# A two-part graph network on one core: settling stages fed from the attentions ahead, records saved and reloaded, marks joined on TensorE

## The chip, the cores and the metric

The kernel runs on one core of one Trainium2 chip. The metric is the device time of one execution in microseconds (us). Engines are named as the profile names them: PE is TensorE, DVE is VectorE, ACT is ScalarE, POOL is GpSimd, SP is SyncE, which here only issues transfers.

## What is computed

x has 1250 rows of 768 numbers, the graph 20000 edges (src, dst, one of 34 types). The first part is a network of two GATv2 layers (eight heads, then one), the second a relational layer with an ordinary graph convolution behind it:

```python
def gatv2(x, src, dst, Ws, bs, Wd, bd, attn):
    H, D = attn.shape
    fs = (x @ Ws + bs).reshape(-1, H, D)
    fd = (x @ Wd + bd).reshape(-1, H, D)
    e = leaky_relu(fs[src] + fd[dst], 0.2)
    logits = einsum('ehd,hd->eh', e, attn)
    alpha = softmax of logits over the edges of one dst
    out = segment_sum(alpha[:, :, None] * fs[src], dst, num_segments=N)
    return elu(out)
...
h0 = relu(layernorm(x))
h = layer_norm(gatv2(h0, first weights) + h0, ln1_w, ln1_b)
x = x + layer_norm(gatv2(h, second weights), lno_w, lno_b)
h = relu(layernorm(x))
mean[r, n] = mean of h[src] over the edges of type r into n
h1 = sum over r of mean[r] @ W_rel[r] + h @ W_root + b_rgcn
x = x + gcn(h1 @ W_gcn) + b_gcn
```

## The kernel before, in words

The nodes are ranked by degree and stand in NT = 10 tiles of 128 rows. The edges of a tile are worked off in groups: a group is S = 4 edges for each of 128 nodes. There are 48 groups in 12 turns of U = 4, and three more at the ends whose slots are empty. The kernel is a chain of stages with a barrier between them (`stage`); each engine has its own instruction stream, and semaphores order the streams inside a stage.

1. **Sorting and projection** (up to 323 us): ranks, edge records in `by_dst_d`, then fs and fd for the first layer. Marks of the (type, source) pairs that occur are scattered into four DRAM tables `marked_d`, in part here, in part in the first settling stage (`mark`, L520 to L526).
2. **First attention** (`attention`, L826, from 323.8 us). POOL first gathers all ten tiles of fd (L884), waits for them, and then runs `gather_edges` (L754): it makes `next`, `step` and `slot`, fetches the records of three groups (`record`, L768 to L773), the rows of two (`rows`, L775 to L778), and goes into its loop of turns, which gathers the record of group u+3 and then the four row sets of group u+2. VectorE clears its tables (L977 to L985), adds fs and fd (`add`, L990), makes the softmax arguments (`arguments`, L1033, first line L1041) and the weights; ACT sums and scales; TensorE adds rows (L942, L944) and sums weighted rows (L965).
3. **First settling stage** (`settle(True)`, L1304). SP loads two layer norm vectors, attr and two biases by broadcast to all partitions, then two weights (L1403 to L1410). VectorE waits for all five vectors (L1565) before anything else. For each of ten tiles it divides by the denominators (`rden`, L1622), takes the smaller of this and 0 (L1626), lets ACT make the exponential, adds (L1629), adds h0, normalises (L494 to L503, L1643 to L1647); TensorE transposes and multiplies (L480, L487), VectorE adds the bias. `twice` (L1388) orders the tiles. POOL gathers and scatters the rows and sets 60 of the 160 marks.
4. **Single attention** (`attention_single`, L1089). The same with one head; VectorE counts the edge types per node too (`count`, L1268), and a Signal `read` tells POOL when a record may be overwritten (L1272, L807).
5. **Second settling stage** (`settle(False)`). VectorE waits for four vectors (L1565), makes `rden` (L1568), the counts per type (L1577 to L1581), waits for the four mark tables (L1583), joins them by three maxima (L1585), makes a running sum (L1586) and from it the tables of the relation stage, with two trips to TensorE (L1545 to L1549) and a store of `seen_d` by SP. Then come the ten tiles. A tile has one `o`, `low`, `y` and `mv`; the next one starts behind it (L1619). It has two normalisations: L503 ends each; after the second ACT copies y (L1515), makes the ReLU (L1518) and copies the transposes (L1522), and VectorE adds the bias to the product (L1681).
6. **Relations** (1942 to 2943 us) and **aggregation** (`gather_edges` with `keep_ends`, L2008): rows of y_d are gathered by edge; POOL casts the records to `ends` (L799), VectorE makes weights from them (L2088 to L2109) and adds weighted rows (L2115).
7. **Last stage**: product, graph convolution, output.

## Time and profile before

| | us |
|---|---|
| median of 3 runs | 3665.88 (3660.69 to 3670.1) |
| the profiled execution | 3660.05 |
| its span, from the first to the last instruction | 3658.2 |
| PE busy | 2852.5 (78%) |
| DVE busy | 2403.2 (66%) |
| ACT busy | 1807.4 (49%) |
| POOL busy | 1770.9 (48%) |
| mean granted TensorE clock | 0.889 of full |

The page of the profile gives busy time by engine, the span in 40 slices, the costliest groups of instructions and the chain that ended last. In a kernel of stages such sums are averages over parts with different limits, so the rows further down are from single stages. A line of a timeline is: start, duration, engine, line of the kernel, operation, output and inputs, count, and in brackets how long the engine was idle before it and what released it. "issue" stands for time in which the engine waited for nothing that the profile shows.

### The profile page before, as it was taken

Reading aid. Unit: us, or ns where it says so; the run is one execution under the profiler, and the core shown is the slowest. Engines: PE = TensorE matmul, PEld = TensorE weight load, DVE = VectorE, ACT = ScalarE, POOL = GpSimd, SP = SyncE. Lnnn points to the kernel's source line nnn. Section 1 sums busy time; section 2 is a strip of 40 time slices with the busy share of each in tenths; the row PEclk is TensorE's granted clock in tenths of the full one; section 3 lists DMA queues with packets and bytes.
Section 4 is the critical chain, followed back from the end, with each engine's and each line's share of the span. In section 5 each row is a group of like instructions: output and inputs, shape, how many; then the busy total and the mean of one; then the engine's idle time right before and its main releaser. Section 6 shows DMA issues by size and latency. Waiting matters only on the chain. (4 is left out here: it accounts for less than half of the span.)

```text
span 3658.2 us, 59690 instructions
## 1 busy us (share of the span) xinstructions
PE 2852.5 (78%) x12846; PEld 2109.5 (58%) x12847; DVE 2403.2 (66%) x4964; ACT 1807.4 (49%) x5370; POOL 1770.9 (48%) x2270
## 2 busy tenths in 40 slices
PE   0495888888779799997476999999999934444699
PEld 0253444444445455553246999999999924444455
DVE  5233988898766788887564655555555569999312
ACT  0011888888722122221243656565566648888300
POOL 1574454544446666664012554455444557777000
PEclk6797999999989899999678999999999966666899
DMA  1334444443321455555126777777776545555200
GB/s 34 111 95 133 125 122 122 122 122 122 117 88 44 149 157 157 157 157 157 47 77 208 241 246 249 231 237 245 245 237 228 187 149 177 174 173 176 105 13 29
DMA packets 153631, 545.35 MB, mean 149 GB/s; under 512 B 35106, under 2 KB 36118, under 8 KB 153281
## 3 DMA queue, kind: packets, MB, share of 16 engines
q0 software_dynamic: 85344, 371.14, 32.6%
q1 hardware_dynamic: 47938, 127.49, 10.7%
q10 hardware_dynamic: 20304, 46.21, 4.0%
q8 instruction: 17, 0.28, 0.0%
q14 instruction: 28, 0.23, 0.0%
HBM read 461.45 MB, written 83.59 MB: 149 GB/s over the span
## 5 line engine op out<-in xcount | busy, mean ns | idle before, releaser
L1921 PE MATMUL pO<-wh,gT 128*128 128x384 f32 x3264 | 867.4, 339 | 15.5 <-ACT gT L1872 13.6
L777 POOL DMA_INDIRECT row<-fs_d,rec x400 | 443.3, 1108 | 351.2 <-PE pA L965 188.2
L1921 PEld LDWEIGHTS pO<-wh,gT 128*128 128x128 f32 x3264 | 594.8, 189 | 24.0 <-ACT gT L1872 20.5
L1921 PE MATMUL pO<-wl,gT 128*128 128x384 f32 x1632 | 547.7, 336 | 0.0
L487 PE MATMUL pO<-wt,hT 128*128 128x384 f32 (+1 forms) x1200 | 417.9, 510 | 40.9 <-ACT hT L1522 19.6
L1935 DVE TENSOR_SCALAR cntge<-pT 128x768 int32<-128x768 int32 x137 | 131.2, 958 | 421.4 <-PE pT L480 231.2
L2044 PE MATMUL pC<-identb,own 128*128 128x128 bf16 x960 | 193.8, 305 | 233.7 <-DVE counts L2074 107.4
L903 ACT ACTIVATE sj<-sj 128x96 f32<-128x96 f32 x1176 | 313.1, 268 | 100.0 <-DVE sj L1020 98.4
L487 PEld LDWEIGHTS pO<-wt,hT 128*128 128x128 f32 (+1 forms) x1200 | 235.7, 199 | 213.4 <-issue 65.9
L1872 ACT ACTIVATE gT<-cntge 128x256 fp32r<-128x256 f32 x822 | 296.8, 411 | 32.0 <-DVE cntge L1938 4.3
L1921 PEld LDWEIGHTS pO<-wl,gT 128*128 128x128 f32 x1632 | 308.3, 189 | 0.0
L942 PE MATMUL pS<-row,ident 128*128 128x384 f32 x400 | 184.5, 546 | 128.3 <-DVE sj L1020 90.3
L1198 PE MATMUL pA<-row,share 128*128 128x384 f32 x768 | 256.3, 487 | 0.0
L2044 PEld LDWEIGHTS pC<-identb,own 128*128 128x128 bf16 x960 | 115.2, 143 | 243.5 <-issue 67.7
L965 PE MATMUL pA<-row,ident 128*128 128x384 f32 x768 | 255.5, 486 | 0.0
L777 POOL DMA_INDIRECT row<-y_d,rec x200 | 211.6, 1058 | 66.5 <-issue 61.2
L2022 ACT ACTIVATE far<-nrow,source 128x1280 bf16<-128x1280 f32 x144 | 196.1, 1362 | 90.3 <-DMA row<-y_d,rec 43.6
L525 POOL DMA_INDIRECT marked_d<-marks,recc x160 | 200.0, 1250 | 68.5 <-issue 56.6
L1797 POOL DMA_INDIRECT g<-hr_d,gindex x138 | 168.2, 1219 | 121.6 <-POOL keys L1794 59.0
L903 ACT ACTIVATION_READ_ACCUMULATOR sj<-sj 128x1 f32 x1176 | 220.0, 187 | 2.4 <-issue 2.2
L772 POOL DMA_INDIRECT rec<-by_dst_d,index x153 | 188.2, 1230 | 47.0 <-issue 30.9
L1198 PEld LDWEIGHTS pA<-row,share 128*128 128x128 f32 x768 | 146.7, 191 | 102.8 <-issue 2.0
(351 smaller groups left out, 5837.0 us busy)
## 6 DMA issues: line engine op xcount, KB each, us to landing
fdt<-in_L_gnn_W_rel_dram SPq DMA_DIRECT2D x170, 384.0 KB
startrow<-seen_d ACTq DMA_DIRECT2D x141, 320.0 KB
raw<-in_L_gnn_W_rel_dram SPq DMA_DIRECT2D x34, 384.0 KB
row<-fs_d,rec POOLq DMA_INDIRECT x400
kept_d<-fdt SPq DMA_DIRECT2D x10, 384.0 KB
kept<-kept_d SPq DMA_DIRECT2D x1, 3840.0 KB
fs_d<-of SPq DMA_DIRECT2D x9, 388.0 KB
fd_d<-of SPq DMA_DIRECT2D x9, 388.0 KB, 2.7
```

The lines of the kernel that those rows point to most:

```text
L487: last = pe.matmul(dst[0:rows, q, 0:HALF], rows_t[:, c * P:c * P + rows], w[:, c, lo:up], start=c == 0, stop=c == KC - 1)
L525: pool.indirect_dma_start(marked_d[k], bass.IndirectOffsetOnAxis(ap=keys, axis=0), marks[0:EP], None)\
L772: pool.indirect_dma_start(b["rec"][u][:], None, table_rows, bass.IndirectOffsetOnAxis(ap=b["index"][u][:], axis=0)).then_inc(b["rec_in"][u ...
L777: pool.indirect_dma_start(b["row"][u][:, j, :].bitcast(words), None, table, bass.IndirectOffsetOnAxis(ap=b["rec"][u][:, 2 * j + field:2 * ...
L903: last = act.activation(of_head, of_head, ACT.Copy, accum_out=dots[off % U][:, j, h:h + 1])
L942: pe.matmul(pS[j][:, q, 0:HALF], ident[:], row[off % U][:, S // 2 + j, lo:up], start=True, stop=False)
L965: last = pe.matmul(pA[:, q, 0:HALF], share, row[u][:, j, lo:up], start=j == 0, stop=j == S - 1)
L1198: last = pe.matmul(pA[u % 2][:, q, 0:HALF], share[u % 2][:, 1 + j, :], row[u][:, j, lo:up], start=j == 0, stop=False)
L1872: act.activation(gT[:, c].bitcast(F32R), cut[:, :, c * P:(c + 1) * P], ACT.Copy).then_inc(gT_ok.sem, 1)
L1921: last = pe.matmul(pO[:, q, 0:HALF], gT[:, c, half, :].bitcast(F32R), w[:, c, lo:up].bitcast(F32R), start=c == 0 and k == 0, stop=c == KC ...
L2022: act.activation(far[:], of_node[:], ACT.Square, bias=source[u % 2][:, j:j + 1], scale=-1.0)\
L2044: last = pe.matmul(pC[u % 2][:, c // 4, (c % 4) * P:(c % 4 + 1) * P], equal[u % 2][j][:, c * P:(c + 1) * P], identb[:], start=j == 0, stop ...
```

## The change

- **Ahead.** A new class holds a weight (768 x 768) and two layer norm vectors in SBUF. SP loads them behind its other work in the attention; the settling stage that follows uses them. The first gets Wos, ln1_w and ln1_b, the second W_root, lno_w and lno_b.
- **fd.** In the first attention POOL gathers tile 0 of fd first, the other nine behind the first eight row gathers.
- **Records.** `gather_edges` is split. In the first attention SP writes each group's record to `groups_d` (`save_records`); in the single attention and the aggregation SP reads them from there (`load_records`), and POOL gathers rows only (`gather_rows`). POOL's casts to `ends` are gone; VectorE reads the integer records and signals `read`.
- **settle** is written out as `settle_first` (as before, but for the loads) and `settle_last`.
- **settle_last.** Two sets of `o`, `low`, `y`, `mv`. VectorE starts the next tile inside the present one and evacuates the one before at its end. The four mark tables are joined by accumulating matmuls with the identity on TensorE and a Sign on ACT, between tile 0 and tile 1. The running sum, the tables and the counts stand behind the tiles on VectorE.

The diff, cut to its core:

```diff
+        groups_d = dram("groups_d", (MAX_TURNS * U + U - 1, P, S * 2), I32)
...
+        def gather_edges(pool, b, table, used, between):
+            count_slots(pool, b)
...
             for u in range(ROWS_AHEAD):
                 pool.wait_ge(b["rec_in"][u], 16)
-                rows(u)
-            turns = pool.value_load(ctl[0:1, C_TURNS:C_TURNS + 1], min_val=1, max_val=MAX_TURNS)
+                rows_of(pool, b, u, table, 0, F32)
+            between()
+            turns = turns_of(pool)
...
                     rows_wait(pool, b, i, u - 1)
-                    if read is not None:
-                        read.wait(pool, i, u - 1)
+                    pool.wait_ge(b["saved"][w], i * 16 + 16 * ((u + U - 1) // U))
...
+        def save_records(sp, b):
+            turns = turns_of(sp)
+            with sp.Fori(0, turns) as i:
+                for u in range(U):
+                    sp.wait_ge(b["rec_in"][u], i * 16 + 16)
+                    sp.sem_inc(b["sp_posted"], 1)
+                    sp.dma_start(groups_d[ds(i * U + u, 1)].rearrange("o p c -> p (o c)"), b["rec"][u][:]).then_inc(b["saved"][u], 16)
...
+        def load_records(sp, b):
+            for u in range(U - 1):
+                sp.dma_start(b["rec"][u][:], groups_d[u]).then_inc(b["rec_in"][u], 16)
+            turns = turns_of(sp)
+            with sp.Fori(0, turns) as i:
+                for u in range(U):
+                    rows_wait(sp, b, i, u - 1)
+                    sp.sem_inc(b["sp_posted"], 1)
+                    b["read"].wait(sp, i, u - 1)
+                    sp.sem_inc(b["sp_posted"], 1)
+                    w = u + U - 1
+                    sp.dma_start(b["rec"][w % U][:], groups_d[ds(i * U + w, 1)].rearrange("o p c -> p (o c)"))\
+                      .then_inc(b["rec_in"][w % U], 16)
...
+        def gather_rows(pool, b, table, field, used, words=F32):
+            count_slots(pool, b)
...
+                for u in range(U):
+                    w = u + ROWS_AHEAD
+                    pool.wait_ge(b["rec_in"][w % U], i * 16 + 16 * (w // U + 1))
+                    used.wait(pool, i, w - U)
+                    pool.sem_inc(b["posted"], 1)
+                    rows_of(pool, b, w % U, table, field, words)
...
+        class Ahead:
...
+            def load(self, sp):
+                weight, lnw, lnb = (io[n] for n in self.names)
+                sp.dma_start(self.wt[:], w_view(weight)).then_inc(self.w_in, 16)
+                sp.dma_start(self.lnw[:], lnw.partition_broadcast(P)).then_inc(self.v_in, 16)
+                sp.dma_start(self.lnb[:], lnb.partition_broadcast(P)).then_inc(self.v_in, 16)
...
                         sp.dma_start(attr[:], attn.rearrange("h d -> (h d)").partition_broadcast(P)).then_inc(att_in, 16)
+                        save_records(sp, b)
+                        ahead.load(sp)
...
-                            for t in range(NT):
-                                pool.indirect_dma_start(fdt[:, t, :], None, fd_table, bass.IndirectOffsetOnAxis(
-                                    ap=permc[:, t:t + 1], axis=0)).then_inc(fd_in, 16)
-                            pool.wait_ge(fd_in, 16 * NT)
-                        pool.sem_inc(init_ok, 1)
-                        gather_edges(pool, b, fs_d[0:N], 0, summed)
+                        def others():
+                            for t in range(1, NT):
+                                fd_rows(t)
+                        fd_rows(0)
+                        gather_edges(pool, b, fs_d[0:N], summed, others)
...
                         add(0, 0, 0)
+                        pe.wait_ge(init_ok, 1)
+                        pe.wait_ge(fd_in, 16 * (NT - 1))
...
-                        dve.wait_ge(init_ok, 2)
+                        dve.wait_ge(fd_first, 16)
...
                         add(0, 0, 0)
+                        dve.wait_ge(fd_in, 16 * (NT - 1))
                         turns = dve.value_load(ctl[0:1, C_TURNS:C_TURNS + 1], min_val=1, max_val=MAX_TURNS)
...
+                        load_records(sp, b)
+                        ahead.load(sp)
                         sp.wait_ge(att_in, 16)
...
-                        gather_edges(pool, b, fs_d[0:N], 0, summed, read=read)
+                        gather_rows(pool, b, fs_d[0:N], 0, summed)
```

In `settle_first` SP loads attr, the two biases and Wod only; VectorE waits for them ahead of its first evacuation, TensorE for Wod ahead of its second product. `settle_last`, by engine:

```diff
+                        for k in range(MARKS):
+                            sp.dma_start(marked[:, k, :], marked_d[k].rearrange("(r s) o -> r (s o)", r=RELS)).then_inc(present_in, 16)
+                        sp.dma_start(bias[:], io["L1_gnn_b_rgcn"].partition_broadcast(P)).then_inc(b_in, 16)
...
+                        def rows(i, b):
+                            root(i, b, 2)
+                            affine_ok.wait(act, i, b)
+                            act.activation(ht[b][:], y[b][:], ACT.Relu, bias=mv[b][:, 3:4], scale=mv[b][:, 2:3])\
+                               .then_inc(h_ok.sem, 1)
+                            act.activation(of_tile(fdt, i, b)[:, 0:D], y[b][:], ACT.Copy).then_inc(kept_ok.sem, 1)
+                            t_ok.wait(act, i, b)
+                            prod_ok.wait(act, i, b - 2)
+                            act.activation(split(hT[b][:]), halves(pT), ACT.Copy).then_inc(hT_ok.sem, 1)
...
+                        exp(0, 0)
+                        tile(0, 0, (0, 1))
+                        act.wait_ge(summed, 1)
+                        act.activation(marked[:, 0, :], p_join[0:RELS].rearrange("p q f -> p (q f)")[:, 0:NP], ACT.Sign)\
+                           .then_inc(joined, 1)
...
+                        pe.wait_ge(present_in, 16 * MARKS)
+                        for q, lo, up in ((0, 0, 512), (1, 512, 1024), (2, 1024, NP)):
+                            for k in range(MARKS):
+                                last = pe.matmul(p_join[0:RELS, q, 0:up - lo], ident[0:RELS, 0:RELS], marked[:, k, lo:up],
+                                                 start=k == 0, stop=k == MARKS - 1)
+                        last.then_inc(summed, 1)
+                        turn(0, 0)
...
+                        product(4, 0)
+                        turn(4, 1)
+                        pe.wait_ge(rel_const, 6)
+                        pe.wait_ge(ntiles_ok, 1)
+                        pe.matmul(p_ends[0:RELS, RELS:RELS + 1], upto[:], ntiles[:], start=True, stop=True)
+                        pe.matmul(p_ends[:, 0:RELS], ntiles_all[:], upto[:], start=True, stop=True).then_inc(ends_ok, 1)
+                        product(4, 1)
+                        pe.wait_ge(behind_ok, 1)
...
+                            row_stats(dve, v, y[b], stats, mv[b], P)
+                            dve.sem_inc(var_ok.sem, 1)
...
+                                begin(v, *following)
+                            root_ok.wait(dve, i, b, 1)
...
+                            if behind is not None:
+                                evacuate(*behind)
...
+                        with dve.Fori(0, 4) as i:
+                            tile(i, 1, (i + 1, 0), (i, 0))
+                            tile(i + 1, 0, (i + 1, 1), (i, 1))
+                        tile(4, 1, None, (4, 0))
+                        dve.wait_ge(joined, 1)
+                        pre.link(dve.tensor_tensor_scan(seen_keys, marked[:, 0, :], marked[:, 0, :], 0.0, ALU.add, ALU.max))
```

And in the aggregation:

```diff
-                    gather_edges(pool, b, y_d, 1, used, keep_ends=True, words=I32)
+                    gather_rows(pool, b, y_d, 1, used, words=I32)
...
-                            b["valid"].wait(dve, i, u)
+                            dve.wait_ge(b["rec_in"][u], i * 16 + 16)
...
                             v.link(dve.tensor_tensor(ge[:], over(ends[:, :, 1], 2, shape),
                                                      over(relbase[:], 1, shape), ALU.is_ge))
+                            dve.sem_inc(b["read"].sem, 1)
                             v.link(dve.tensor_tensor(of_rel[:], ge[:, :, 0:RELS], ge[:, :, 1:RELS + 1],
                                                      ALU.subtract))
```

## Rows read from the trace of the kernel before

**Rows 1.** Busy us by stage, columns PE, PEld, DVE, ACT, POOL, then clock, DMA share, GB/s
```profile
323.80:996.30 672.50, 549.23 (x1568) 309.20 (x1568) 579.02 (x1169) 555.22 (x3180) 333.91 (x366) 0.93 0.41 125
...
1201.50:1718.10 516.60, 458.94 (x1360) 259.55 (x1360) 439.48 (x1365) 137.88 (x349) 327.12 (x356) 0.96 0.53 155
...
1718.10:1942.60 224.50, 116.47 (x308) 66.24 (x308) 127.89 (x240) 62.57 (x79) 26.97 (x48) 0.73 0.21 75
```

**Rows 2.** Timeline, start of the first attention: start us, us, engine, line, idle before
```profile
323.82 1.00 POOL L884 DMA_INDIRECT fdt<-fd_d,permc  x1 [38.69 <-POOLq L139]
...
339.84 0.19 POOL L760 COPY next<-first_row 128x11 int32<-128x11 int32 x1 [3.72 <-DMA fdt<-fd_d,permc]
...
340.24 0.17 DVE L977 COPY left<-degr 128x11 f32<-128x11 f32 x1 [21.11 <-POOLq L765]
...
346.30 0.95 POOL L777 DMA_INDIRECT row<-fs_d,rec  x1 [0.31 <-issue]
...
354.58 1.83 DVE L1001 TENSOR_TENSOR sj<-row,fdt 128x768 f32<-128x768 f32 x2 [2.00 <-DMA row<-fs_d,rec]
...
365.58 0.23 DVE L1041 TENSOR_SCALAR neg<-slot,left 128x4 f32<-128x4 f32 x1 [1.20 <-ACT sj L903]
```

**Rows 3.** Timeline, end of the first attention and start of the first settling stage
```profile
966.45 0.98 POOL L772 DMA_INDIRECT rec<-by_dst_d,index  x1 [0.47 <-issue]
...
988.78 5.32 PE L965 MATMUL pA<-row,ident 128*128 128x384 f32 x16
...
996.28 0.36 SPq L1403 DMA_DIRECT2D lnw<-in_L_gnn_ln_w_dram  x1
...
1008.44 0.20 DVE L1568 TENSOR_SCALAR rden<-den 128x80 f32<-128x80 f32 x1 [13.07 <-DMA bias<-in_L_gnn_bod_dram]
```

**Rows 4.** Timeline of the single attention, VectorE, its start and a turn's start
```profile
1216.56 1.83 DVE L1232 TENSOR_TENSOR leak<-row,fdt 128x768 f32<-128x768 f32 x2 [0.22 <-DMA row<-fs_d,rec]
...
1468.53 0.23 DVE L1254 TENSOR_SCALAR val<-slot,left 128x4 f32<-128x4 f32 x1 [1.51 <-issue]
```

**Rows 5.** Waits, 1240 to 1700 us: who waited for what, us in total, times, longest
```profile
PE pS L1180 <- DMA row<-fs_d,rec: 34.1, 36, 2.3
```

**Rows 6.** Timeline of the second settling stage, its start and its last tile
```profile
1727.55 0.17 DVE L1568 TENSOR_SCALAR rden<-den 128x10 f32<-128x10 f32 x1 [16.48 <-DMA bias<-in_L_gnn_b_rgcn_dram]
...
1734.19 1.22 SPq L1420 DMA_DIRECT2D marked<-marked_d  x4
...
1749.93 4.52 DVE L1585 TENSOR_TENSOR marked<-marked 34x1280 f32<-34x1280 f32 x3 [15.04 <-DMA marked<-marked_d]
...
1754.49 2.82 DVE L1586 TENSOR_TENSOR_SCAN startrow<-marked 34x1280 f32<-34x1280 f32 x1
...
1762.22 1.20 PE L1549 MATMUL p_tile<-behind,ntiles_all 34*128 34x300 f32 x2
...
1765.26 0.96 DVE L1622 TENSOR_TENSOR o<-acc,rden 128x768 f32<-128x768 f32 x1
...
1911.91 0.96 DVE L1622 TENSOR_TENSOR o<-acc,rden 128x768 f32<-128x768 f32 x1 [0.95 <-ACT ht L1518]
...
1916.51 0.96 DVE L1629 SCALAR_TENSOR_TENSOR o<-o,low 128x768 f32<-128x768 f32 x1 [3.04 <-ACT low L1508]
...
1926.27 0.16 DVE L503 SCALAR_TENSOR_TENSOR mv<-mv 128x1 f32<-128x1 f32 x1
...
1930.78 9.91 PE L487 MATMUL pO<-wt,hT 128*128 128x384 f32 x24 [0.90 <-ACT hT L1522]
...
1940.73 0.96 DVE L1681 TENSOR_TENSOR acc<-pO,bias 128x768 f32<-128x768 f32 x1 [13.19 <-PE pO L487]
```

**Rows 7.** Timeline of the aggregation, VectorE, within one group of edges
```profile
3201.98 0.89 DVE L2098 TENSOR_SCALAR own<-nrow,source 128x1280 bf16<-128x1280 f32 x1 [0.16 <-DVE source L2096]
3202.78 0.30 DVE L2101 TENSOR_TENSOR ge<-ends,relbase 128x140 f32<-128x140 f32 x1
3203.11 0.30 DVE L2103 TENSOR_TENSOR of_rel<-ge 128x136 f32<-128x136 f32 x1
```

653 lines of the change are left out of this document (378 added, 275 removed).

## The prediction

> **What bounds the kernel now.** I read the page first, for the loops, then the busy times stage by stage, then the timeline at each border between stages, and last the waits inside the loops.
>
> Busy times by stage [rows 1]: VectorE works 579 of 672 us in the attention of eight heads and 439 of 517 us in the single one, but only 128 of 224.5 us in the second settling stage, where TensorE works 116. That stage is bound by a chain that passes between engines, not by an engine.
>
> Borders. The first attention begins with ten gathers of fd, a wait for them, then the records and rows; VectorE's first addition comes 30.8 us after the first gather, and the softmax of the first group 11.0 us later [rows 2]. The first settling stage opens with a VectorE wait of 13.07 us for the broadcast vectors [rows 3]. The second opens with the same wait (VectorE's first work is at 1727.55), then waits 15.04 us for the marks, and starts its first tile at 1765.26 [rows 6]. From there a tile takes (1911.91 - 1765.26)/9 = 16.3 us [rows 6].
>
> Inside the single attention the only wait on VectorE that lasts is 1.51 us of register loads, once a turn of four groups [rows 4]. TensorE waits for rows [rows 5], but has time left.
>
> **The change, part by part.** The profiled execution took 3660.05 us, span 3658.2; the median of the runs shown is 3665.88. The sum is against 3660, and I apply it to the median. What a measurement can tell from no change is 0.3%, 11 us.
>
> *fd behind the first rows.* POOL issued ten gathers from 323.82 to 336.12, where its wait begins, one each 1.23 us. With one fd gather ahead, the slot numbers are ready at about 325.4 in place of 340.0; VectorE's memsets last 12.3 us (340.24 to 352.58, where its wait for rows begins) and end at about 338.1. POOL repeats 339.84 to 354.58 (14.7 us from the first copy to the rows being there) from about 325.6, so the first addition comes at 340.3, 14.3 us sooner [rows 2]. But nine fd gathers follow the eight of rows: eight begin at 332.1, nine at 342.1, issued by 353.1, and landed 3.7 us later, as in the row of L760: 356.8. VectorE waits for them ahead of its turn loop, behind which stand the softmax arguments of group 0 and all that ACT and TensorE do for it; its register loads (1.5 us) come behind that wait. So the softmax starts at 358.3 in place of 365.58: **-7.3**. Bounds: -14.3 if the loads and the wait hide, -4 if the seventeen gathers land more slowly than issued. POOL reaches its loop 3 us sooner, and group 2's rows keep their lead.
>
> *Saving the records.* SP writes 51 records of 4 KB; POOL waits for that before it overwrites a buffer whose record came several us earlier. VectorE sets this loop, POOL does not (334 of 672 us busy [rows 1]): 0, and at most 51 issues' worth of POOL's spare time. The weights wait on SP behind the last save: the last record is gathered at 966.45 [rows 3], so they leave at about 972, 24 us before the stage ends; late next would be the last row gather, if they crowd it.
>
> *First settling stage.* VectorE waits for nothing at its start. SP begins at 996.28; VectorE's six semaphore openings take some 0.8 us, so 997.1 in place of 1008.44: **-11.3** [rows 3]. What is late next: three broadcasts and Wod, 3.5 MB. At the pace of the five vectors before (2 MB by 1008.44) they are there by 1018, and TensorE wants Wod only behind a first tile and a first product, 12 and 10 us as in [rows 6], about 1022. The gather of h0's rows has 4 us less cover, so I leave -8 to -12. The tiles behind run as before.
>
> *Single attention.* POOL loses per group two small operations and a record gather, SP gets a load and two waits. VectorE's own loop is unchanged. At the start, memsets and rows end together (VectorE waits 0.22 us for rows [rows 4]), and the memsets stay: **0**, between -2 and +2.
>
> *Second settling stage.* The first tile no longer waits for broadcasts, marks or tables: VectorE starts it at 1720, not 1765.26. Tile 0 takes at most the 14.5 us of the last one (1911.91 to the end of L503, 1926.43). Then, in tile 1, it stalls. ACT's queue holds, between tile 0 and tile 1, the copy of tile 0's transposes and the Sign of the joined marks; TensorE does the join first. Four mark loads are there 15.7 us after their issue (1734.19 to 1749.93), so at 1733.9. The join is 12 matmuls over 5120 columns [rows 6]: at the pace of the last product (12 x 384 columns in 9.91 us, begun on an idle TensorE) 11.0 us; at the pace of L1549 (300 columns in 1.20 us) 20.5; at that of L965 (8 x 384 columns in 5.32 us [rows 3]) 8.9. L1549 ran behind an idle TensorE and L965 in a busy stretch, 4.0 and 1.7 ns a column: near the two levels of the granted clock, 1.2 and 2.4 GHz, whose mean is 0.73 of full in this stage [rows 1]. I take 12, nearest to the product, which gives 1746; transposes, copy and Sign add 3.9 (my estimate, from the 4.35 us between L503 and the last product, which hold two copies, a ReLU and the transposes): 1749.9. Tile 1 has two thirds of its 9.9 us left from there: 1756.5. For the period: 9.9 us from L1629 to the end of L503 (1916.51 to 1926.43), the next tile's first two operations 1.6 (1911.91 to 1916.51, less 3.04 of wait), evacuation 1.0, less the 0.3 wait for the root, and 0.7 of semaphore and register work: 12.9 us, against 16.3. The last product (9.9 us) has to fit behind the way through ReLU, transposes and copy, 4.35 us less the 0.8 of the other copy, which now stands behind; that makes 13.5, so it just fails to fit at half clock and fits at the full one. Eight tiles less one opening: 101.5, so 1858. Then the tables, once ahead of the tiles, stand behind them: 10.8 us from the scan to the first tile (1754.49 to 1765.26), with TensorE's last product, 9.9, and two evacuations put in between, less 1 that overlaps; VectorE's count sums (7.3 us, 1727.55 to 1734.89, with the reciprocal of the denominators) lie beside that product. End at 1879.5 in place of 1941.7: **-62**. Bounds: -74 (full clock) and -40 (join at 20.5 and a period of 14.5).
>
> *Aggregation.* POOL's casts go; they were not what VectorE waited for. VectorE gets one more semaphore increment per group. Such an increment stands ahead of L2098: VectorE is idle 0.16 us there, against 0.03 between the end of L2101 and L2103, where none stands [rows 7]. VectorE has no other idle time there, so 48 x 0.13 = **+6**; bounds 0 and +8. The Trainium skill, VectorE: DVE Perf Modes, The DRAIN you can't avoid, says a semaphore after each operation costs nothing extra. By that rule this term would be 0 and the sum 6 us lower. It speaks of increments carried by an operation, and the row of a separate one disagrees.
>
> Sum: -7.3 - 11.3 - 62 + 6 = -74.6: 3585.5 against 3660.05, 3591 on the median.
>
> **The rivals.**
> *Less overlap.* Two tiles share one pT and one pO, and ACT and TensorE take their work in order. If that holds the period at 15 to 16.3 us, eight tiles cost 17 to 27 more: about 3616. For it: the product nearly fails to fit. Against: each wait I can follow is met with a us to spare.
>
> *The rows set the single attention.* TensorE waited 34.1 us for rows in 460 us [rows 5], and POOL's next record waits for VectorE's read. If that drives VectorE, freeing POOL gives up to 34: 3557. Against: VectorE's waits don't name rows, sums or TensorE [rows 4]. The Trainium skill, SBUF — State Buffer, SBUF: two separate sides, says a gather issued by GpSimd can't write its descriptors while VectorE holds the port they share. The record loads leave that path for SP's, so by this rule too the way to the rows gets shorter.
>
> *Slower.* Both later gather loops now get their records from SP, behind two waits and a round trip through DRAM in 32-byte pieces. If a record comes later than POOL wants it by d per group, 96 groups pay 96 d; the gain is gone at d = 0.78 us, and d = 1.5 gives 3735. For it: it is a new wait in front of every row gather. Against: a record is asked for a whole group, 9 to 10 us, before its rows are. The Trainium skill, DMA: Bandwidth & Descriptors, Specifications, warns of transfers under 512 bytes, handled by read-modify-write; by this rule SP's 4 KB writes would be slow, but no row here shows a price.
>
> *The prefetch doesn't land.* If SP is still held by its last waits when the attention ends, both settling stages load as before: 11 us lost in the first and up to 8 in the second: 3605.
>
> **How the numbers follow.** Forecast as summed 0.62 (3591), less overlap 0.15 (3616), rows 0.07 (3557), prefetch late 0.08 (3605), slower 0.04; 0.04 for two small losses at once that leave no measurable change. The forecast's own bounds add up to about -95 and -45 if all fall one way; independent ones to some -88 and -52. The range 3563 to 3625 takes in the forecast, less overlap and late prefetch, and leaves out the slow rival and the far end of the rows. Faster by over 0.3%: 0.92; within: 0.04; slower: 0.04.
>
> **What would show it.** In the profile after: VectorE's first addition at about 340 and softmax at 358; no wait for a broadcast at either settling start; between tiles 0 and 1 of the second a VectorE wait of 9 to 11 us for ACT's root; a tile period near 12.9 us; TensorE's last product between the two table matmuls; the single attention as long as before; aggregation 6 us longer, with 0.16 us behind L2101's successor. A tile period over 15 us, row waits on VectorE, or POOL waiting for records would prove me wrong.

## The result and the profile after

The kernel after took 3608.39 us (median of 4 runs, 3602.33 to 3609.28) against 3667.99 us of the kernel before (4 runs, 3660.69 to 3671.18): a ratio of 0.9837, with a 95% interval of 0.9818 to 0.9856. That is 59.6 us less; the prediction was 75 less (3591, range 3563 to 3625), so the measured time lies 17 us above the forecast and inside its range. The profiled execution took 3608.54 us with a span of 3606.6; the one before, 3660.05, was the shortest of its runs, so the two profiles differ by 51.6 us and not by 59.6. What follows splits those 51.6.

Busy times by stage in the kernel after (columns as in [rows 1]: PE, PEld, DVE, ACT, POOL, clock, DMA share, GB/s): first attention, single attention, second settling stage.

```profile
323.87:999.61 675.74, 556.18 (x1568) 312.11 (x1568) 578.88 (x1169) 554.28 (x3180) 338.38 (x366) 0.92 0.43 129
1197.00:1714.85 517.85, 461.29 (x1360) 261.11 (x1360) 440.99 (x1365) 135.39 (x349) 233.27 (x200) 0.96 0.55 161
1714.85:1890.60 175.75, 123.86 (x332) 65.43 (x332) 119.54 (x237) 63.59 (x80) 25.61 (x46) 0.78 0.22 74
```

The second settling stage does the same work in 175.75 us that took 224.5. The two attentions are as long as they were, though GpSimd does 94 us less in the single one. The account, from the timelines of both kernels:

| part | before, us | after, us | difference | predicted |
|---|---|---|---|---|
| first attention, first fd gather to last addition | 671.55 | 674.77 | +3.2 | -7.3 |
| from there to the first work of the single attention | 207.21 | 199.24 | -8.0 | -11.3 |
| single attention | 515.52 | 516.97 | +1.5 | 0 |
| second settling stage | 224.5 | 175.75 | -48.8 | -62 |
| relations, up to the clearing of the counts | 1004.4 | 1003.6 | -0.8 | 0 |
| aggregation, to its last addition of counts | 465.36 | 466.59 | +1.2 | +6 |
| the rest | | | 0 | 0 |

**Start of the first attention.** The timeline answers to [rows 2]; the last row is of TensorE.

```profile
323.87 1.00 POOL L956 DMA_INDIRECT fdt<-fd_d,permc  x1 [39.56 <-POOLq L141]
340.80 1.83 DVE L1079 TENSOR_TENSOR sj<-row,fdt 128x768 f32<-128x768 f32 x2 [3.35 <-DMA row<-fs_d,rec]
360.23 0.23 DVE L1119 TENSOR_SCALAR neg<-slot,left 128x4 f32<-128x4 f32 x1 [9.49 <-issue]
363.20 0.27 DVE L1130 COPY top<-mnew 128x8 f32 x1 [1.19 <-issue]
368.17 0.96 DVE L1079 TENSOR_TENSOR sj<-row,fdt 128x768 f32<-128x768 f32 x1 [4.71 <-issue]
379.25 0.23 DVE L1119 TENSOR_SCALAR neg<-slot,left 128x4 f32<-128x4 f32 x1 [0.20 <-issue]
...
358.99 1.62 PE L1018 MATMUL pS<-row,ident 128*128 128x384 f32 x2 [11.09 <-issue]
```

The first addition is 13.8 us sooner, the softmax arguments of group 0 are 5.4 us sooner, and those of group 1 come later than before, at 379.25 against

```profile
378.30 0.23 DVE L1041 TENSOR_SCALAR neg<-slot,left 128x4 f32<-128x4 f32 x1 [0.20 <-issue]
```

TensorE stood 11 us at the same wait for the nine gathers as VectorE and did its sums for group 1 only from 358.99, beginning at half clock; before, it had done them while VectorE was still on group 0. VectorE then stops twice (1.19 and 4.71 us) where nothing in the trace releases it. TensorE's sums are ready at 367.2, before VectorE comes back at 368.17, so in this profile the stops took the lead and not the late sums.

**End of the first attention**, answering to [rows 3]:

```profile
985.10 0.91 PE L1018 MATMUL pS<-row,ident 128*128 128x384 f32 x2 [3.79 <-DMA row<-fs_d,rec]
...
992.05 5.32 PE L1043 MATMUL pA<-row,ident 128*128 128x384 f32 x16
997.68 0.96 DVE L1108 TENSOR_TENSOR acc<-pA,scaled 128x768 f32 x1 [7.65 <-PE pA L1043]
999.61 0.33 SPq L1457 DMA_DIRECT2D attr<-in_L_gnn_attno_dram  x1
1000.21 0.20 DVE L1388 TENSOR_SCALAR rden<-den 128x80 f32<-128x80 f32 x1 [1.56 <-PEq L141]
1008.58 0.96 DVE L1584 SCALAR_TENSOR_TENSOR y<-o,hg 128x768 f32<-128x768 f32 x1 [2.23 <-DMA hg<-h_d,gindex]
```

The last group's 16 matmuls start at 992.05 in place of 988.78. The settling stage then starts 0.6 us behind its border with no broadcast to wait for, and waits 2.23 us for the gathered rows of h0.

**Second settling stage**, answering to [rows 6]:

```profile
1714.85 1.24 SPq L1675 DMA_DIRECT2D marked<-marked_d  x4
1716.23 0.72 DVE L1828 TENSOR_SCALAR o<-acc,rden 128x768 f32<-128x768 f32 x1
1734.36 17.28 PE L1797 MATMUL p_join<-marked,ident 34*34 34x512 f32 x24 [21.42 <-DMA marked<-marked_d]
1736.29 0.96 DVE L1841 SCALAR_TENSOR_TENSOR o<-o,low 128x768 f32<-128x768 f32 x1 [5.23 <-DMA bias<-in_L_gnn_b_rgcn_dram]
...
1753.15 0.81 ACT L1758 ACTIVATE hT<-pT 128x768 f32<-128x768 f32 x1 [20.23 <-PE pT L482]
1753.85 1.22 ACT L1772 ACTIVATE marked<-p_join 34x1280 f32<-34x1280 f32 x1
1755.20 0.17 DVE L504 RECIPROCAL mv<-mv 128x1 f32<-128x1 f32 x1 [13.98 <-ACT mv L1744]
1763.84 0.96 DVE L1834 TENSOR_TENSOR acc<-pO,bias 128x768 f32 x1 [2.09 <-PE pO L489]
...
1857.13 0.96 DVE L1834 TENSOR_TENSOR acc<-pO,bias 128x768 f32 x1 [0.28 <-DVE mv L505]
1871.55 0.96 DVE L1834 TENSOR_TENSOR acc<-pO,bias 128x768 f32<-128x768 f32 x1 [3.54 <-PE pO L489]
1876.88 9.64 PE L489 MATMUL pO<-settle_wt,hT 128*128 128x384 f32 x24
1886.64 0.96 DVE L1834 TENSOR_TENSOR acc<-pO,bias 128x768 f32<-128x768 f32 x1 [1.76 <-PE pO L489]
```

VectorE starts its tiles at once. In tile 1 it waits 13.98 us for ScalarE's root, because the root stands behind the copy of tile 0's transposes and the Sign, and these stand behind the join on TensorE: 17.28 us. After that the evacuations are (1857.13 - 1763.84)/7 = 13.3 us apart, and the last product lies between the two table matmuls.

**Waits for rows** on TensorE in the single attention, 1236 to 1696, answering to [rows 5]:

```profile
PE pA L1279 <- ACT share L1245: 28.9, 16, 3.9
PE pS L1261 <- DMA row<-fs_d,rec: 5.4, 9, 1.7
```

Of the 34.1 us for rows 5.4 are left. 28.9 us for ScalarE stand in the place of the rest.

### The profile page after: what moved, and what is told of

It is laid out like the page before. It is cut to its first block and busy times, and to the rows that moved or that the text cites. A ratio compares the mean times of both kernels' runs of the same rounds, so it can differ in the third digit from the quotient of the medians.

```text
span 3606.6 us, 59098 instructions
## 1 busy us (share of the span) xinstructions
PE 2867.7 (80%) x12870; PEld 2109.7 (58%) x12871; DVE 2393.1 (66%) x4961; ACT 1802.2 (50%) x5371; POOL 1545.8 (43%) x1910
## 5 line engine op out<-in xcount | busy, mean ns | idle before, releaser
L759 POOL DMA_INDIRECT row<-y_d,rec x200 | 202.9, 1014 | 248.9 <-DVE acc L2343 198.9
L1279 PE MATMUL pA<-row,share 128*128 128x384 f32 x768 | 265.6, 500 | 30.7 <-ACT share L1245 30.7
L489 PE MATMUL pO<-wt,hT 128*128 128x384 f32 (+1 forms) x720 | 238.3, 490 | 22.1 <-DMA attr<-in_L_gnn_attn_dram 12.9
L489 PEld LDWEIGHTS pO<-wt,hT 128*128 128x128 f32 (+1 forms) x720 | 135.7, 190 | 119.4 <-issue 31.4
L1043 PEld LDWEIGHTS pA<-row,ident 128*128 128x128 f32 x768 | 145.9, 190 | 101.8
```

The lines of the kernel that those rows point to most:

```text
L489: last = pe.matmul(dst[0:rows, q, 0:HALF], rows_t[:, c * P:c * P + rows], w[:, c, lo:up], start=c == 0, stop=c == KC - 1)
L759: pool.indirect_dma_start(b["row"][u][:, j, :].bitcast(words), None, table, bass.IndirectOffsetOnAxis(ap=b["rec"][u][:, 2 * j + field:2 * ...
L1043: last = pe.matmul(pA[:, q, 0:HALF], share, row[u][:, j, lo:up], start=j == 0, stop=j == S - 1)
L1279: last = pe.matmul(pA[u % 2][:, q, 0:HALF], share[u % 2][:, 1 + j, :], row[u][:, j, lo:up], start=j == 0, stop=False)
```

## The experiments

Every kernel below is the kernel after with the edit named. Whole times scatter: the one with fd gathered ahead gave 3605 to 3625 in four runs, and the relations, whose code is the same everywhere, took between 1006 and 1016 us. So verdicts rest on lengths of stages, each from one profile. These scatter too: where the second settling stage has the same code, "settling 2" took 171.1 to 174.7 us in eight profiles, "single" 512.7 to 520.1 in all of them. The column "start" runs from the first fd gather to the softmax arguments of group 1, "attention" to the last addition, "settling 1" from there to its last copy of fd, "single" from the first work of that attention to the first work of the next stage, and "settling 2" from there to the start of its last evacuation (for the kernel before counted from 0.5 us behind SP's first issue, as in the others).

| kernel | start | attention | settling 1 | single | settling 2 | aggregation | median, us | ratio to before (95%) |
|---|---|---|---|---|---|---|---|---|
| before | 54.5 | 671.6 | 204.9 | 516.0 | 222.1 | 465.4 | | |
| after | 55.4 | 674.8 | 197.0 | 517.5 | 171.3 | 466.6 | 3608.4 | 0.9837 |
| after, again | 56.3 | 672.4 | 196.8 | 517.9 | 173.7 | 466.5 | 3609.0 | 0.9849 (0.9824-0.9873) |
| fd ahead | 59.4 | 676.1 | 196.5 | 519.4 | 171.9 | 466.4 | 3619.2 | 0.9864 (0.9839-0.9889) |
| no prefetch | 54.9 | 673.0 | 203.8 | 513.7 | 174.3 | 466.7 | 3617.0 | 0.9870 (0.985-0.989) |
| join on VectorE | 56.7 | 674.7 | 197.3 | 517.4 | 156.7 | 466.2 | 3600.2 | 0.9826 (0.981-0.9843) |
| own records | 57.0 | 675.5 | 196.6 | 516.9 | 171.5 | 465.4 | 3612.8 | 0.9854 (0.9838-0.9871) |
| two fd rows ahead | 42.8 | 665.1 | 196.5 | 518.0 | 174.0 | 466.7 | 3600.4 | 0.9827 (0.9811-0.9844) |
| join on VectorE, bias first | 50.0 | 667.9 | 197.2 | 513.2 | 157.0 | 466.2 | 3589.1 | 0.9803 (0.9786-0.9821) |
| nothing saved | 49.9 | 668.3 | 196.9 | 516.7 | 174.7 | 464.7 | 3604.0 | 0.9839 (0.9816-0.9862) |
| join warmed up | 50.0 | 668.0 | 197.0 | 520.1 | 168.4 | 466.4 | 3605.5 | 0.9843 (0.9823-0.9863) |
| tiles kept warm | 56.3 | 672.6 | 196.4 | 516.9 | 150.3 | 466.1 | 3586.0 | 0.9788 (0.976-0.9816) |
| earlier prefetch | 58.1 | 674.1 | 195.8 | 512.7 | 171.1 | 466.1 | 3608.1 | 0.9851 (0.9819-0.9883) |
| all three | 50.7 | 669.1 | 196.9 | 514.0 | 150.7 | 468.0 | 3586.5 | 0.9785 (0.9764-0.9805) |

**1. fd gathered ahead of the records again.**

```diff
 fd_rows(0)
-gather_edges(pool, b, fs_d[0:N], summed, others)
+others()
+pool.wait_ge(fd_first, 16)
+pool.wait_ge(fd_in, 16 * (NT - 1))
+gather_edges(pool, b, fs_d[0:N], summed, lambda: None)
```

> The kernel after, with all ten rows of fd gathered ahead of the records, as in the kernel before. My theory: the lead of 14.5 us that the new order gives at the first addition (340.8 against 354.6) is lost before the second group is done, because TensorE, VectorE and ScalarE stand behind one wait for the nine other gathers (until about 358) and start again on cold queues; VectorE then reaches the softmax of group 1 at 379.25 against 378.30 in the kernel before. So undoing it costs nothing: first addition at 354.6, softmax of group 0 at 365.6, softmax of group 1 at about 378.3, and a time within 2 us of the kernel after (3606 to 3610). Rival: the new order does give its 7.3 us and the loop loses them later to the saving of the records; then the stage ends 7 us later than in the kernel after and the time is about 3615.

The start took 59.4 us, 4 us more than in the kernel after, not the same; the stage ended 1.3 us later, not 7. Neither forecast holds, and the time, 3619.2 us, is above both. The new place of fd does give something, but 59.4 is also 4.9 more than the kernel before had with the same order of gathers, and here too VectorE stopped 3.22 us without a releaser. So the next question was the saving.

**2. Nothing saved.** No records are written; both later loops gather their own (experiment 6 has that part alone).

```diff
-pool.wait_ge(b["saved"][w], i * 16 + 16 * ((u + U - 1) // U))
...
-sp.dma_start(groups_d[ds(i * U + u, 1)].rearrange("o p c -> p (o c)"), b["rec"][u][:]).then_inc(b["saved"][u], 16)
```

> The kernel after, but no records are saved: the single attention and the aggregation gather their own, and in the first attention SP writes nothing and GpSimd waits for no save; the prefetch leaves when the last record is there. The fd gathers stand as in the kernel after. From the first fd gather to the softmax of group 1 the kernel before took 54.5 us, the kernel after 55.4, and the one with fd gathered ahead and records saved 59.4. My theory: the saving costs about 4 us at the loop's start (its writes of 32 bytes a partition go through the same DMA engines as the first rows and the engines' code) and the new place of fd gives about as much back; without the saving the softmax of group 1 comes 50 to 52 us after the first fd gather. Rival: the saving costs nothing; then it stays at 55 to 57.

49.9 us, at the lower edge of my theory's window, and yet the theory falls: two kernels that ran beside it on the same chip and save every record (join on VectorE with the bias first, join warmed up) had 50.0. There, saving costs nothing. The first of the two shows the start without the stops, against the same lines of the kernel after above:

```profile
360.83 0.23 DVE L1119 TENSOR_SCALAR neg<-slot,left 128x4 f32<-128x4 f32 x1 [9.49 <-issue]
...
363.08 1.83 DVE L1079 TENSOR_TENSOR sj<-row,fdt 128x768 f32<-128x768 f32 x2 [0.30 <-issue]
374.72 0.23 DVE L1119 TENSOR_SCALAR neg<-slot,left 128x4 f32<-128x4 f32 x1 [0.20 <-issue]
```

Its wait for fd is as long (9.49 us), but the first pass through the loop runs on. Here VectorE does wait for TensorE's late sums, 1.07 us. Where the stops are absent, the new place of fd gives 54.5 - 50.0 = 4.5 us. Where they are present it gives 59.4 less about 56.4 = 3, a weak reading: 59.4 is one profile, and the seven others with stops have starts from 54.9 to 58.1. Whether a kernel that saves nothing would have them on the chips that show them was not tried.

**3. Two rows of fd ahead, the wait for the other eight inside the loops.**

```diff
-.then_inc(fd_first if t == 0 else fd_in, 16)
+.then_inc(fd_first if t < 2 else fd_in, 16)
...
 add(0, 0, 0)
-dve.wait_ge(fd_in, 16 * (NT - 1))
...
 arguments(v, i, u, t[u + 1])
+if u == 1:
+    dve.wait_ge(fd_in, 16 * (NT - 2))
 add(i, u + 1, t[u + 2])
```

(and the same for TensorE, ahead of its sums for the third group)

> The kernel after, but two rows of fd are gathered ahead of the records and eight behind the first rows, and the wait for those eight stands inside the loops, ahead of the addition of the third group, not ahead of the loops. My theory: the wait ahead of the loops holds three engines until about 358; with it gone the softmax of group 0 starts about 353 (first addition 342, plus 11 as in the kernel before), the softmax of group 1 at about 366 to 368 against 379.25, and the lead stays to the end of the stage: 8 to 11 us off the first attention. Rival: the loop's start is held by the crowd of gathers itself (the operations behind it show idle times of 4.7 and 1.2 us without a releaser), not by the wait; then the softmax of group 1 stays at 376 or later and the stage gives 3 us or less.

The start took 42.8 us, 7.2 less than the kernels beside it and as forecast: the wait ahead of the loops was the cost. But the stage is only 2.9 us shorter (665.1 against 668.0), where I had forecast 8 to 11. The rest is lost one group later, on TensorE and VectorE:

```profile
366.88 1.64 PE L1019 MATMUL pS<-row,ident 128*128 128x384 f32 x2 [10.68 <-DMA row<-fs_d,rec]
...
375.15 0.96 DVE L1100 SCALAR_TENSOR_TENSOR sj<-pS,attr 128x768 f32<-128x768 f32 x1 [1.48 <-PE pS L1021]
380.42 0.96 DVE L1110 TENSOR_TENSOR acc<-pA,scaled 128x768 f32 x1 [2.46 <-PE pA L1045]
```

The rows of the third group are gathered behind the eight of fd, and TensorE takes them up at half clock. A queue of 25 gathers of about 1.25 us each has to be worked off in any order.

**4. No prefetch in the first attention.**

```diff
 save_records(sp, b)
-ahead.load(sp)
...
 def _(sp):
+    ahead.load(sp)
...
```

> The kernel after, but the first Wos and the two norm vectors are loaded at the start of the first settling stage and not behind the saved records. My theory: the 2.9 MB of the prefetch crowd the last row gather of the attention; in the kernel after TensorE waits 3.79 us for it (985.10 against 983.51) and then runs at half clock, so the stage ends at 999.6 against 996.3. Without the prefetch TensorE takes up the last group at 983.5 and the stage ends 3.3 us sooner, at 996.3; the settling stage then waits 5 to 10 us for vectors and weights, so the time is 2 to 7 us above the kernel after (3610 to 3615). Rival: the late end comes from the saving of the records, not from the prefetch; then the stage still ends at 999.6 and the time is 5 to 10 us above.

The settling stage took 203.8 us, 6.8 more; VectorE waits 9.95 us in it for a norm vector. The time, 3617.0 us, is 2 above my forecast. The end of the attention did not come back to that of the kernel before: TensorE's wait was 2.22 us, as before, but it went on at half clock all the same:

```profile
985.46 1.65 PE L1017 MATMUL pS<-row,ident 128*128 128x384 f32 x2 [2.22 <-DVE sj L1097]
986.90 1.49 PE L1019 MATMUL pS<-fdt,ident 128*128 x2
988.18 1.16 PE L1017 MATMUL pS<-row,ident 128*128 128x384 f32 x2
989.17 0.81 PE L1019 MATMUL pS<-fdt,ident 128*128 x2
```

Two matmuls of 0.81 us at full clock take 1.65, 1.49 and 1.16 here. The kernel before had the same 2.2 us gap and kept its clock. So of the 3.3 us at the end, 1.6 are a late row gather and 1.7 the clock. The saving is not the cause either: the kernel that saves nothing has the same 2.21 us gap and the same half clock behind it.

**5. The prefetch earlier**, between the loop of saves and the last three.

```diff
+between()
 for u in range(U - 1):
     sp.wait_ge(b["rec_in"][u], turns * 16 + 16)
...
-save_records(sp, b)
-ahead.load(sp)
+save_records(sp, b, lambda: ahead.load(sp))
```

> The kernel after, but the prefetch for the first settling stage stands between the loop that saves the records and the three last saves, so it leaves about two turns' worth of groups sooner. My theory: the prefetch costs little where it stands (in the kernel without it the attention took 673.0 us, with it 668.0 to 674.8), so the attention takes 667 to 674 us and the settling stage the same 197 us from its end to its last tile. Rival: the prefetch crowds the last row gather by the 3.3 us that the profile of the kernel after shows; then TensorE's wait for rows ahead of the last group (3.79 us there) goes down to the 2.2 us that it waits for VectorE anyway, in a profile in which the others of this code show it too.

TensorE waited 2.20 us for VectorE ahead of the last group, not for a row, and the attention took 674.1 us. But the join on VectorE, with the prefetch where the kernel after has it, shows the same 2.2 us and no wait for a row. Of the eleven profiles with the prefetch in its old place three have a wait for a row there: 3.79 us in the kernel after, 3.33 in experiment 3, and in the kernel after repeated

```profile
984.72 0.91 PE L1018 MATMUL pS<-row,ident 128*128 128x384 f32 x2 [2.31 <-DMA row<-fs_d,rec]
```

So the late row gather comes in some executions and not in others, and is worth 1.6 us at most. That the prefetch makes it late fits these profiles, all with the prefetch, but is not shown.

**6. Own records in both later loops**, gathered by GpSimd with the function of the kernel before.

```diff
-load_records(sp, b)
...
-gather_rows(pool, b, fs_d[0:N], 0, summed)
+gather_both(pool, b, fs_d[0:N], 0, summed, read=read)
...
-gather_rows(pool, b, y_d, 1, used, words=I32)
+gather_both(pool, b, y_d, 1, used, keep_ends=True, words=I32)
```

> The kernel after, but the single attention and the aggregation gather their records on GpSimd again, as in the kernel before (the first attention still saves them, for nobody). My theory: VectorE sets both loops, so who fetches the records costs nothing; the separate semaphore increment in the aggregation (0.12 us a group) is nearly paid back by the small wait it replaces (0.10 us a group, the gap ahead of the operation on source). Single attention within 1.5 us of 517.9, aggregation 1 us shorter, time within 3 us of 3608. Rival: the relief of GpSimd bought time in the single attention that something else took away; then the single attention gets 5 us or more longer. Second rival: records from SP come late; then it gets 5 us or more shorter.

The single attention took 516.9 us against 517.5, within the 512.7 to 520.1 that this stage shows with the same code. TensorE's waits for rows come back in full and cost nothing:

```profile
PE pS L1329 <- DMA row<-fs_d,rec: 34.3, 38, 2.4
```

The aggregation took 465.4 us, as before; with the loaded records it takes 466.1 to 468.0. The time, 3612.8 us, is 5 above my forecast of 3608; the stages that this edit touches don't show that difference.

**7. The join on VectorE, behind the last tile.**

```diff
-last = pe.matmul(p_join[0:RELS, q, 0:up - lo], ident[0:RELS, 0:RELS], marked[:, k, lo:up],
-                 start=k == 0, stop=k == MARKS - 1)
...
-act.activation(marked[:, 0, :], p_join[0:RELS].rearrange("p q f -> p (q f)")[:, 0:NP], ACT.Sign)\
-   .then_inc(joined, 1)
...
-tile(4, 1, None, (4, 0))
-dve.wait_ge(joined, 1)
+tile(4, 1, None, None)
+dve.wait_ge(present_in, 16 * MARKS)
+for k in range(1, MARKS):
+    pre.link(dve.tensor_tensor(marked[:, 0, :], marked[:, 0, :], marked[:, k, :], ALU.max))
+evacuate(4, 0)
```

> The kernel after, but the marks are joined by VectorE with three maxima behind the last tile, where it waits 3.54 us for a product, in place of 24 matmuls on TensorE ahead of the tiles. My theory: the join (17.3 us at half clock, begun when the marks are there at 1734.4) is all that holds tile 1. Without it VectorE waits in tile 1 only for the broadcast of the bias (5.2 us, until 1736.3), the 14.0 us of wait for ScalarE's root are gone, and the three maxima (4.6 us) cost about 1 us at the end: 13 us less, 3595. Rival: TensorE's transposes and product of tile 0 (1.5 + 0.8 + 9.6 us) stand in the same queue, and the wait only moves on to the evacuation of tile 0; then the gain is 5 us or less.

The stage took 156.7 us, 14.6 less. In tile 1 only the wait for the bias is left. The time was 3600.2 us, 8 less than the kernel after, where I expected 13. The saving in the stage is the surer reading.

**8. The same with the bias loaded ahead of the marks.**

```diff
+sp.dma_start(bias[:], io["L1_gnn_b_rgcn"].partition_broadcast(P)).then_inc(b_in, 16)
 for k in range(MARKS):
     sp.dma_start(marked[:, k, :], marked_d[k].rearrange("(r s) o -> r (s o)", r=RELS)).then_inc(present_in, 16)
-sp.dma_start(bias[:], io["L1_gnn_b_rgcn"].partition_broadcast(P)).then_inc(b_in, 16)
```

> The kernel with the join on VectorE, and in it the bias of the second settling stage is loaded ahead of the four loads of marks. That kernel's second settling stage took 159.3 us from its first operation, 14.6 less than the kernel after's 173.9, and VectorE waits in it about 5 us for the bias in tile 1. My theory: the bias is late only because it stands behind the marks; with it first the wait goes and the stage gives 4 to 5 us more: about 154.5 us. Rival: the broadcast takes its 20 us wherever it stands, or ScalarE and TensorE are no further in tile 1 anyway; then the stage stays at 158 to 160.

The wait for the bias is gone, but the stage took 157.0 us, as without this edit: the rival holds. TensorE's rows of this kernel:

```profile
1749.48 1.54 PE L482 MATMUL pT<-ident,ht 128*128 128x128 f32 x6 [4.31 <-ACT ht L1753]
1752.00 10.91 PE L489 MATMUL pO<-settle_wt,hT 128*128 128x384 f32 x24 [0.98 <-ACT hT L1758]
1762.75 0.82 PE L482 MATMUL pT<-ident,ht 128*128 128x128 f32 x6
1764.47 8.01 PE L489 MATMUL pO<-settle_wt,hT 128*128 128x384 f32 x24 [0.90 <-ACT hT L1758]
```

Every second product begins behind 4.31 us of idle time and takes 10.91 us, the next one 8.01. The evacuations alternate between 12.7 and 14.6 us. Against the kernel of experiment 7 the first evacuation comes 3.1 us sooner, and the seven steps behind it take 94.7 us in place of 91.5. So it was 3 us that was won in tile 1, and the products at half clock took them back, as far as one profile of each can tell.

**9. The join warmed up**: the join of the kernel after, with 90 matmuls that nobody reads ahead of it.

```diff
+for _ in range(90):
+    pe.matmul(p_join[:, 0, 0:P], ident[:], ident[:], start=True, stop=True)
 pe.wait_ge(present_in, 16 * MARKS)
```

> The kernel after, but TensorE runs 90 matmuls of 128 columns that nobody reads while it waits for the marks, so that the join does not start on an idle engine. My theory: the join's 17.3 us are columns at the lower level of the clock (24 matmuls, 5120 columns, 3.4 ns a column); on a busy TensorE it takes 9 to 10 us, the Sign comes 7 to 8 us sooner and the stage is about 7 us shorter (167). Rival: the length is set by the shape (34 rows, a change of weights each time), not by the clock; then it stays above 15 us and the stage as long as it is.

The join took 12.1 us, between the two forecasts, and the stage 168.4, below the 171.1 to 174.7 that it takes without this edit. The granted clock (the third figure from the end, ahead of DMA share and GB/s) shows why:

```profile
1711.20:1731.50 20.30, 20.24 (x180) 20.17 (x180) 11.68 (x26) 7.70 (x9) 5.58 (x13) 1.00 0.44 140
1731.50:1735.50 4.00, 4.00 (x11) 1.09 (x11) 2.90 (x6) 0.00 (x0) 0.00 (x0) 1.00 0.16 64
1735.50:1739.50 4.00, 4.00 (x8) 0.88 (x7) 1.18 (x2) 0.00 (x0) 0.00 (x0) 0.66 0.00 0
1739.50:1743.50 4.00, 4.00 (x9) 1.26 (x7) 0.00 (x0) 0.00 (x0) 0.00 (x0) 0.50 0.00 0
```

It starts at full clock, as the dummies left it, and falls to half in the middle of the join, while TensorE is busy all the time with matmuls of 34 rows by 34 columns of weights.

**10. TensorE kept busy between the products** of the kernel with join on VectorE and bias first.

```diff
+def keep_busy():
+    for _ in range(12):
+        pe.matmul(p_join[:, 0, 0:P], ident[:], ident[:], start=True, stop=True)
...
 product(i, 0)
+keep_busy()
 turn(i, 1)
 product(i, 1)
+keep_busy()
 turn(i + 1, 0)
```

> The kernel with the join on VectorE and the bias first, and in it TensorE runs 12 matmuls of 128 columns that nobody reads (about 2.7 us) behind every product of the second settling stage, where it would otherwise stand idle. There every second product began behind 4.3 us of idle time and took 10.9 us, the others began without it and took 8.0, and the evacuations came 12.74 and 14.55 us apart in turn. My theory: the difference is the granted clock, so with TensorE kept busy all products take 8.0 us, all evacuations come 12.74 us apart, and the stage from its first operation to its last evacuation takes 157.0 - 4 x 1.8 - 2 x 2.7 = about 144.5 us. Rival: the extra matmuls only delay the transposes behind them, since TensorE gets its tile later than they end; then the stage stays at 155 or gets longer.

(The trace has two records for each of these fp32 matmuls, so x24 stands for the 12.) The next eight products take 8.0 us each, and the first eight evacuations are 12.7 to 12.9 us apart:

```profile
1745.69 8.01 PE L489 MATMUL pO<-settle_wt,hT 128*128 128x384 f32 x24 [0.90 <-ACT hT L1758]
1753.53 2.84 PE L1787 MATMUL p_join<-ident 128*128 128x128 f32 x24
...
1758.01 8.00 PE L489 MATMUL pO<-settle_wt,hT 128*128 128x384 f32 x24 [0.98 <-ACT hT L1758]
```

The stage took 150.3 us (150.7 in experiment 11): 6.7 less, where I expected 12.5. The two last evacuations stayed at 15.6 and 15.1 us, and the last product takes 9.57 us: TensorE had stood idle for 4.8 us just before it, but for two small table matmuls.

**11 and 12. All three edits that help (3, 8, 10), beside the kernel after.**

> The kernel after with what the other runs recommend: two rows of fd ahead and the wait for the rest inside the loops, the join on VectorE behind the tiles with the bias loaded first, and TensorE kept busy between the products of the second settling stage. My theory: the parts add up, 3 us in the first attention and 21 us in the second settling stage (150.3 against 171.3), so it is 22 to 26 us faster than the kernel after on the same chip, about 3584. Rival: what is won in the first attention is lost again in its loop, since the third group's rows come late; then the gain is the settling stage's 19 to 21 us alone.

> The kernel after, unchanged, beside the run above on the same chip. Its medians of the first measurement were 3608.4 for 3668.0 of before. My theory: 3606 to 3611. From the first fd gather to the softmax of group 1 it showed 55.4 us, while two kernels with the same first attention showed 50.0 on another chip: if that is a matter of the chip, it stands near 50 or near 56 together with nothing else changed; if of the single execution, it can be anything between.

3586.5 us against 3609.0 on the same chip: 22.5 less, inside my 22 to 26. But the kernel without experiment 3's edit had 3586.0 on the same chip, so that edit shows in no whole time, as the rival says. In the profiles the second settling stage is 23.0 us shorter than in the kernel after repeated (150.7 against 173.7), and the attention 3.3 (669.1 against 672.4). The rival's reason, late rows of the third group, costs nothing in this profile: VectorE had lost more before them. In the start this kernel took 50.7 us, not the 42.8 of experiment 3: VectorE stopped 7.54 us ahead of the softmax of group 0, for which the trace names no engine of this core. The kernel after repeated its time, and its start took 56.3 us, with the two stops (1.24 and 6.09 us).

## Why the prediction was right, and where it was off

The sign, the main part and the range (3563 to 3625) held. The sum was 15 us too large on the medians and 23 on the two profiles (74.6 against 51.6), and that it was not worse is in part luck: an error of 4.8 us the other way, in the aggregation, covers some of it. The time, 3608.4, lies nearer to the rival of less overlap (3616) than to the forecast (3591). Its mechanism is not what happened: it needs a period of 15 us or more, and the period was 13.3. The prediction's bounds were also added up wrongly: term by term they give about -102 and -42 and not -95 and -45; the stated range, 103 to 41 us below the median before, spans the right ones. Term by term:

**fd behind the first rows: -7.3 predicted, about -3 to -4.5 measured** (experiments 1 and 2), at the near bound; in the kernel after itself the softmax of group 1 came 0.9 us later than before (55.4 against 54.5 from the first gather). The first addition came at 340.8 (forecast 340.3), the softmax of group 0 at 360.2 (forecast 358.3). Two steps of the sum failed. The nine gathers were there 2 us later than forecast (TensorE goes on at 358.99, not 356.8). And I followed VectorE through that wait and left TensorE out: its sums for group 1 stand behind the same wait, and before they had been done ahead of time. Without the stops that costs VectorE 1.07 us. In eight profiles VectorE's stops on the first pass through the loop took more, the longest of each 2.8 to 6.2 us; in the kernel after they took the whole lead. Their cause is open. The Trainium skill, Runtime: NRT & Kernel Launch, Instruction fetch mechanics, says that a taken branch can stall an engine while its code is fetched by DMA. The trace of the kernel after has no packet on a code queue between 358 and 369 us, so it doesn't bear that out.

**End of the first attention: 0 predicted, +3.3 in the profile.** I had named what is late next (the last row gather, crowded by the weights) and priced it at nothing. It is worth up to 1.6 us when it happens; the other 1.7 are TensorE's clock. Neither came when the kernel after was repeated: there TensorE waited 2.31 us and kept its clock.

**First settling stage: -11.3 predicted, -8 measured**, the near bound. VectorE started within 0.6 us of the border; h0's rows took 2.2 us of it, and the first product ran at half clock. Experiment 4 shows the prefetch itself to be worth 6.8 us.

**Saving and loading records, single attention: 0 predicted, within the scatter** (experiments 2 and 6). Both rivals on this part fall. Rows set nothing: of their 34 us of waits 5.4 are left, and VectorE's stage stayed at 517. And SP's records came in time: GpSimd waited for one only at the start of each loop (5.4 us in two waits). The Trainium skill's rule on the port between VectorE and GpSimd (SBUF — State Buffer, SBUF: two separate sides) would let the rows come sooner. They did, and VectorE was not waiting for them; whether by the port or because GpSimd had less to do, no run here tells.

**Second settling stage: -62 predicted, -48.8 measured.** The mechanism is as described, wait by wait: VectorE's stall in tile 1, tiles overlapping, the last product between the tables. One wait was not foreseen: 5.23 us for the broadcast of the bias in tile 1, which the join hides. The sizes were off in two places. The join began 3.7 us later than forecast (against the stage's own start), since the marks took 19.5 us from their first issue in place of 15.7. It took 17.3 us and not 12. I had its bounds from rows at either clock (8.9 and 20.5) and chose the product's pace; the nearer row was L1549's, a small matmul behind an idle TensorE. Together that put tile 1's root at 1755.2 in place of 1746.7 (the forecast 1749.9, shifted with the stage's start). The period was 13.3 us and not 12.9: the text says that the product just fails to fit at half clock, and every second one was at half clock. From the end of tile 1 to that of tile 9 it took 106.3 us (1761.75 to 1868.01) in place of 101.5, 4.8 more. The tail is as forecast, 22.6 us to the end of the stage against 22.4. So 8.5 and 4.8 us make up the 13 that are missing, and experiments 7 and 10 take back 14.6 and 6.7 us from just these two places.

**Aggregation: +6 predicted, +1.2 measured.** The increment costs what I said: behind L2328, in the place of L2101, VectorE is now idle 0.15 us.

```profile
3348.79 0.30 DVE L2328 TENSOR_TENSOR ge<-rec,relbase 128x140 f32<-128x140 int32 x1
3349.24 0.30 DVE L2331 TENSOR_TENSOR of_rel<-ge 128x136 f32<-128x136 f32 x1 [0.15 <-DVE ge L2328]
```

But I overlooked what went. Ahead of the operation on `source` stood the wait for GpSimd's cast of the record, and the start of that operation came 0.18 us behind that of the one before it, now 0.08:

```profile
3389.89 0.15 DVE L2089 TENSOR_SCALAR left<-left  x1
3390.07 0.16 DVE L2094 SCALAR_TENSOR_TENSOR source<-ends,val 128x4 f32<-128x4 f32 x1
```

```profile
3347.38 0.15 DVE L2316 TENSOR_SCALAR left<-left  x1
3347.46 0.16 DVE L2321 SCALAR_TENSOR_TENSOR source<-rec,val 128x4 f32<-128x4 int32 x1
```

0.12 less 0.10 us a group, 48 times, is 1.0 us. Experiment 6 gives the same 0.7 to 1.3 from the other side. The rule of the Trainium skill (VectorE: DVE Perf Modes, The DRAIN you can't avoid) would have put this term at 0 and been nearer to the +1.2 that was measured. The rows still show that a separate increment is not free.

## What to carry to other kernels

When a wait is moved ahead of a loop, list every engine that now stands behind it and what each had done ahead of time. When two tiles are made to overlap, work put once in front of TensorE (a join, a table) delays every engine that feeds on its queue: put it behind the tiles on an engine that waits there anyway. Where a product only just fits into a tile's period, price it at both levels of the clock: here the products took 10.9 us behind a gap of 4.3 us and 8.0 without it.

## What the runs showed of the hardware that was not expected

- **Small matmuls did not keep TensorE's clock.** Busy for 12.1 us without a gap on matmuls with 34 rows and 34 columns of weights, it fell from 1.00 to 0.50 of full speed (2.4 to 1.2 GHz). Busy with 128 by 128 ones it stayed at 1.00.
- **Unread matmuls paid.** 12 of them (2.84 us) in a gap of 4.3 us took the product behind them from 10.9 to 8.0 us and made the stage 6.7 us shorter (one profile of each, on two chips; a second one with them shows 150.7 us again).
- **The same gap of 2.2 to 2.3 us, ahead of the last group of the first attention, cost the clock in some profiles and not in others**: not in the kernel before at 983.5 us (0.81 us for two matmuls behind it), in the kernel after repeated and with the earlier prefetch; it did in seven others, the kernel without the prefetch among them (up to 1.65).
- **On the first pass through its loop VectorE stopped for 2.8 to 6.2 us with nothing that the trace shows to wait for.** It did in eight profiles, one of them with fd ahead of the records, and did not in the kernel before nor in the four kernels that ran together on another chip, three of which save their records. The kernel with all three edits had its stop of 7.54 us in another place. Whether it hangs on the chip, on the execution, or on the two together with the saving was not settled.
